# Controller feed-forward: tie test, pick product and output product each moved within and across the steps of a software pipeline

## The reference

```python
lr = xf @ m1                                            # 128 -> 64
mask_logits = jnp.einsum('bl,lxy->bxy', lr, m2) + mb    # 8 blocks x 64
quant_mask = jnp.argmax(mask_logits, axis=-1)           # one unit in each block
mid = jnp.einsum('ai,aji->aj', xf, w1p[j, quant_mask])
relu = jax.nn.relu(mid)
res = jnp.einsum('ai,aij->aj', relu, w2p[j, quant_mask]) + b2
# outside: x = x + tanh(g_ffn[2]) * res, with xf = layernorm(x)
```

## Time and profile before

| | |
|---|---|
| median of three runs | 1644.13 us (1643.41 to 1644.64) |
| the profiled execution | 1646.58 us |
| its span, first to last instruction | 1644.8 us |
| busy: PE, DVE, ACT, POOL | 1391.0, 1037.0, 716.7, 768.4 us |
| mean granted TensorE clock | 0.931 of full speed |

### The profile page before, as it was taken

One profiled execution on the slowest core, in us unless ns is written; L12 is line 12 of the kernel. 1 busy time (PEld: TensorE's weight loads), 2 busy tenths in 40 slices (PEclk: granted clock), 3 DMA queues, 4 the chain that ended last, 5 costly groups with the idle time before them and its releaser, 6 DMA issues. The chain is left out here.

```text
span 1644.8 us, 34070 instructions
## 1 busy us (share of the span) xinstructions
PE 1391.0 (85%) x10919; PEld 1114.0 (68%) x10919; DVE 1037.0 (63%) x2336; ACT 716.7 (44%) x1767; POOL 768.4 (47%) x989
## 2 busy tenths in 40 slices
PE   4998776989675877999978986999999999687996
PEld 3777556989565555666645546778788787486984
DVE  4887862414387787999958883545565754363555
ACT  2677453323365324565634442544545445221121
POOL 2554581444371444455434442445444676206445
PEclk9999997999856896999979997999999999898998
DMA  7400123758110000000000000000000000375952
GB/s 187 185 1 2 30 88 108 224 174 265 48 42 2 1 1 1 1 0 0 1 1 0 0 0 1 1 0 0 1 1 1 11 17 19 98 218 174 292 154 83
DMA packets 96485, 100.02 MB, mean 61 GB/s; under 512 B 12149, under 2 KB 69677, under 8 KB 95726
## 3 DMA queue, kind: packets, MB, share of 16 engines
q1 hardware_dynamic: 62322, 69.60, 14.0%
q0 software_dynamic: 8192, 16.79, 3.4%
q10 hardware_dynamic: 25852, 12.09, 2.6%
HBM read 72.23 MB, written 26.21 MB: 60 GB/s over the span
## 5 line engine op out<-in xcount | busy, mean ns | idle before, releaser
L445 POOL TENSOR_TENSOR exp_scores<-exp_scores,softmax_recip 128x308 f32<-128x308 f32 x256 | 181.8, 741 | 181.1 <-DVE softmax_recip L614 180.9
L640 PE MATMUL psum<-identity,exp_scores 128*77 128x128 f32 x1024 | 163.6, 286 | 34.2 <-POOL exp_scores L445 21.6
L1966 POOL TENSOR_TENSOR exp_scores_xattn<-exp_scores_xattn,softmax_recip_xattn 128x1640 f32<-128x1640 f32 x32 | 93.5, 2921 | 162.5 <-DVE softmax_recip_xattn L2139 162.5
L1211 PE MATMUL psum<-sorted_transposed_ffn,tile_weights_up_ffn 128*128 128x128 f32 x1280 | 164.2, 283 | 5.0 <-DVE sorted_transposed_ffn L1099 4.7
L1211 PEld LDWEIGHTS psum<-sorted_transposed_ffn,tile_weights_up_ffn 128*128 128x128 f32 x1280 | 153.8, 197 | 11.7 <-DVE sorted_transposed_ffn L1099 11.5
L640 PEld LDWEIGHTS psum<-identity,exp_scores 128*77 128x77 f32 x1024 | 122.5, 152 | 56.7 <-issue 26.3
L985 POOL DMA_INDIRECT gathered_rows_ffn<-sorted_y,slot_ffn x96 | 90.7, 945 | 104.3 <-DMA sorted_y<-expert_rows_ffn 45.7
L460 ACT COPY probs_transposed<-psum 77x512 f32<-77x512 f32 x192 | 111.1, 581 | 52.2 <-PE psum L640 50.6
L1221 PE MATMUL psum<-expert_weights_down_ffn,hidden_ffn 128*128 x960 | 124.4, 281 | 3.4 <-issue 2.8
L974 POOL DMA_INDIRECT sorted_x<-xn_ffn,slot_ffn x64 | 61.3, 958 | 132.3 <-DVE slot_ffn L859 113.4
L1221 PEld LDWEIGHTS psum<-expert_weights_down_ffn,hidden_ffn 128*128 128x128 f32 x960 | 116.6, 196 | 5.8 <-issue 5.8
(11 more groups left out here) (367 smaller groups left out, 3353.4 us busy)
## 6 DMA issues: line engine op xcount, KB each, us to landing
tile_weights_up_ffn<-in_L_ffn_packed_dram SPq DMA_DIRECT2D x160, 256.0 KB, 3.2
sorted_rows_ffn<-sorted_x SPq DMA_DIRECT2D x80, 128.0 KB, 3.5
sorted_y<-expert_rows_ffn ACTq DMA_DIRECT2D x80, 128.0 KB
sorted_x<-zeros SPq DMA_DIRECT2D x4, 1280.0 KB, 13.4
x_residual<-in_x_dram SPq DMA_DIRECT2D x4, 512.0 KB, 11.1
expert_weights_down_ffn<-in_L_ffn_packed_dram SPq DMA_DIRECT2D x8, 256.0 KB, 15.5
sorted_x<-xn_ffn,slot_ffn POOLq DMA_INDIRECT x128, 2.3
gathered_rows_ffn<-sorted_y,slot_ffn POOLq DMA_INDIRECT x128, 2.7
```

The lines of the kernel that those rows point to most:

```text
L445: nc.gpsimd.tensor_tensor(e[:, par, heads, :], e[:, par, heads, :], rec.to_broadcast([S, HG, KC]), ALU.mult).then_inc(s["probs_ready"], 1)
L640: last = nc.tensor.transpose(m.psum[0:KC, 4 + g % 2, h * S:(h + 1) * S], e[:, nxt, g * HG + h, :], m.ident[:, :])
L1211: mm = nc.tensor.matmul(m.psum[:, 2 * (n % 2) + half, to:to + SUB], w[:, n % DEPTH, u, at:at + 128], xst[:, n % 2, u * SUB:(u + 1) * SUB], ...
L1966: nc.gpsimd.tensor_tensor(ev, ev, recip[:, par, :].unsqueeze(2).to_broadcast([S, H3, KV]), ALU.mult).then_inc(s["probs_ready"], 1)
```

## The change

`pipeline_pairs` replaces `pipeline4` in this stage, and `has(b, lag)` says whether batch b - lag exists (always, in the loop); the loop now holds steps 4 to 27 and six steps are written out after it. In the step of batch b the parts are now: transpose, w1's product and low-rank product of b + 1; logits, top, comparison and count multiply of b; code, tie test and product of b - 1; transposes, `rt` copy, w2's product and addition of b - 2; statistics of b - 3. No instruction of a batch is added or removed.

The diff, cut to its core (the engines' loops; waits on buffers follow the new order):

```diff
+def has(b, lag):
+    return not isinstance(b, int) or 0 <= b - lag < B
...
@@ gpsimd
-                    if middle:
+                    if has(b, 0):
                         wait(pool, s["ge_ready"], b + 1)
...
@@ scalar
+                    if has(b, 2):
+                        wait(act, s["rt_in_psum"], b - 1)
+                        wait(act, s["y_done"], b - 2)
+                        nc.scalar.copy(rt[:, :], m.psum[:, 5, :]).then_inc(s["rt_ready"], 1)
...
-                    if back:
-                        wait(act, s["rt_in_psum"], b)
-                        wait(act, s["y_done"], b - 1)
-                        nc.scalar.copy(rt[:, :], m.psum[:, 5, :]).then_inc(s["rt_ready"], 1)
...
@@ vector
+                    if has(b, 0):
+                        wait(dve, s["logits_in_psum"], b + 1)
+                        wait(dve, s["ge_ready"], b)
+                        nc.vector.tensor_reduce(top[:, :], logits, AX.X, ALU.max).then_inc(s["top_ready"], 1)
+                    if has(b, 1):
                         wait(dve, s["coded"], b)
+                        wait(dve, s["first_ready"], b - 1)
                         nc.vector.tensor_reduce(code[:, :], pv, AX.X, ALU.max).then_inc(s["code_ready"], 1)
+                    if has(b, 0):
                         wait(dve, s["top_ready"], b + 1)
                         wait(dve, s["rt_in_psum"], b - 1)
                         nc.vector.tensor_tensor(pick[:, par, :, :], logits, top[:, :].unsqueeze(2).to_broadcast(wide),
                                                 ALU.is_ge).then_inc(s["ge_ready"], 1)
+                    if has(b, 1):
+                        wait(dve, s["code_ready"], b)
+                        nc.vector.tensor_tensor(pv, pv, code[:, :].unsqueeze(2).to_broadcast(wide), ALU.is_equal).then_inc(s["first_ready"], 1)
+                    if has(b, 3):
+                        statistics(b - 3)
+                    if has(b, 1):
                         wait(dve, s["first_ready"], b)
                         wait(dve, s["full_ready"], b)
                         nc.vector.tensor_tensor(pf, pf, full[:, nxt, :], ALU.mult).then_inc(s["picked_ready"], 1)
...
@@ tensor
+                    if has(b, 2):
+                        wait(pe, s["picked_ready"], b - 1)
+                        wait(pe, s["rt_ready"], b - 2)
+                        for c in range(CH):
+                            mm = nc.tensor.transpose(m.psum[:, 5, c * S:(c + 1) * S],
+                                                     pick[:, par, :, :].rearrange("p x y -> p (x y)")[:, c * 128:(c + 1) * 128], m.ident[:, :])
+                        mm.then_inc(s["rt_in_psum"], 1)
+                    if has(b, -1):
+                        wait(pe, s["xt_ready"], b + 2)
+                        wait(pe, s["full_ready"], b)
+                        nc.tensor.matmul(m.psum[:, 3 + nxt, :], xt[:, nxt, :], w1[:, :], start=True, stop=True).then_inc(s["full_in_psum"], 1)
+                        nc.tensor.matmul(m.psum[0:ML, 0, S:2 * S], m1[:, :], xt[:, nxt, :], start=True, stop=True).then_inc(s["low_in_psum"], 1)
+                    if has(b, 2):
                         wait(pe, s["rt_ready"], b - 1)
                         wait(pe, s["x_done"], b - 2)
...
```

More of the change, by code:

```diff
@@ L1711, in _, with pipeline_pairs @@
                 pipeline4(pe, step, NGB)
+def has(b, lag):
+    return not isinstance(b, int) or 0 <= b - lag < B
+def pipeline_pairs(eng, step, n=B):
+    for b in range(-1, 4):
+        step(b, b % 2)
+    with eng.Fori(0, (n - 8) // 2) as i:
+        step(i * 2 + 4, 0)
+        step(i * 2 + 5, 1)
+    for b in range(n - 4, n + 2):
+        step(b, b % 2)
 def controller_feed_forward(nc, m, sem, clear):
@@ L1756, in step @@
                                                 ALU.mult).then_inc(s["coded"], 1)
-                pipeline4(pool, step)
+                pipeline_pairs(pool, step)
             @block.scalar
@@ L1769, in normalise, with step @@
                                          bias=m.shift[:, bass.ds(b, 1)]).then_inc(s["xn_ready"], 1)
-                def step(b, par, front, middle, back, tail):
+                def step(b, par):
                     nxt = 1 - par
-                    if front:
+                    if has(b, -1):
                         wait(act, s["xt_in_psum"], b + 2)
@@ L1776, in step @@
                         nc.scalar.copy(xt[:, nxt, :], m.psum[:, 0, 0:S]).then_inc(s["xt_ready"], 1)
-                    if front and not (isinstance(b, int) and b + 2 >= B):
+                    if has(b, -2):
                         wait(act, s["xt_in_psum"], b + 1)
                         normalise(b + 2, par)
-                    if front:
+                    if has(b, 2):
+                        wait(act, s["rt_in_psum"], b - 1)
+                        wait(act, s["y_done"], b - 2)
+                        nc.scalar.copy(rt[:, :], m.psum[:, 5, :]).then_inc(s["rt_ready"], 1)
+                    if has(b, -1):
                         wait(act, s["low_in_psum"], b + 2)
@@ L1787, in step @@
                         nc.scalar.activation(full[:, par, :], m.psum[:, 3 + par, :], ACT.Relu).then_inc(s["full_ready"], 1)
[L1788 to L1791 removed]
                 normalise(0, 0)
[L1794 removed]
+                pipeline_pairs(act, step)
                 preload(nc, m, ACT.Sqrt)
@@ L1803, in _, with statistics, step @@
                 wide = [S, MX, MY]
-                def step(b, par, front, middle, back, tail):
+                def statistics(b):
+                    wait(dve, s["x_done"], b + 1)
+                    nc.vector.bn_stats(m.moments[:, b, :], m.x[:, b, :])
+                def step(b, par):
                     nxt = 1 - par
-                    pv = pick[:, nxt, :, :]
-                    if back:
+                    logits, pv = m.psum[:, 1 + par, :].rearrange("p (x y) -> p x y", y=MY), pick[:, nxt, :, :]
+                    if has(b, 0):
[3 more added lines that the diff above has]
+                    if has(b, 1):
                         wait(dve, s["coded"], b)
+                        wait(dve, s["first_ready"], b - 1)
                         nc.vector.tensor_reduce(code[:, :], pv, AX.X, ALU.max).then_inc(s["code_ready"], 1)
[L1812 to L1819, removed]
+                    if has(b, 0):
                         wait(dve, s["top_ready"], b + 1)
@@ L1833, in step @@
                                                        ALU.mult, ALU.add).then_inc(s["x_done"], 1)
-                        wait(dve, s["x_done"], b - 1)
-                        nc.vector.bn_stats(m.moments[:, b - 2, :], m.x[:, b - 2, :])
-                pipeline4(dve, step)
+                pipeline_pairs(dve, step)
+                statistics(B - 1)
             @block.tensor
@@ L1861, in step @@
                         mm.then_inc(s["y_done"], 1)
[L1862 to L1876, removed]
+                pipeline_pairs(pe, step)
 def latent_attention(nc, m, sem, r, clear):
```

9 lines of the change are left out of this document (3 added, 6 removed).

## The result

The kernel after takes 1658.45 us (median of 5 runs, 1653.07 to 1659.09) against 1644.13 (1643.41 to 1646.65): ratio 1.0078, 95% interval 1.0062 to 1.0094. It is slower by 14 us; the forecast was 1651.7, range 1645 to 1659. (In later runs the kernel before had medians of 1646.24 and 1647.78; against those the loss is 12 and 11 us.) The mechanism of the steady steps came out as forecast. The larger part of what the stage itself lost is TensorE's clock in the fill and the drain, where the forecast saw less of it or none. The start of the next stage took 2.1 us longer too, but no run ties that to the change.

A forecast was written before the change was run, and what follows sets the result against it. The prediction took the closed ring of VectorE and GpSimd waits, 4.255 us a step, to bound the kernel. Fill +4.1, steps +2.7 and drain +0.8 gave +7.6 on 1644.13, thus 1651.7 us, range 1645 to 1659.

The forecast's parts named there:

- The mechanism of the steady steps: Steady steps: VectorE's product, with two SBUF inputs, waits 1.00 us for GpSimd's multiply; 28 steps give +2.7.
- The ring: Steady step, VectorE and GpSimd waiting for each other: 4.255 us becomes 4.35, +2.7 over 28 steps, bounds 0 to +5.6.
- The faster rival: Steady step: VectorE isn't held, GpSimd pays for both, TensorE's 3.9 bounds; -9.9 in the steps, 1638.3 us, chance 0.12.
- The much slower rival: Steady step: GpSimd's bias addition gets ahead of the waiting product, holding it 0.42 longer; step 4.77, 1664 us, chance 0.08.
- The fill: Stage start to comparison of batch 3: bare w1's product, uncovered copy waits and later clock rise, +4.1, bounds +2.4 to +7.2.
- the one that let the clock rise halfway through TensorE's fourth step: Fill: TensorE's step after batch 2's logits runs half at half clock and takes 3.7 + 1.9 us.
- The drain: Last comparison to end of last statistics: last code starts behind held product and addition, one statistics intervenes; +0.8, 0.5 to 1.2.
- The total: Whole kernel: fill, steps and drain sum to +7.6, giving 1651.7 us, range 1645 to 1659 for 8 in 10.

The follow-up runs named there:

- Experiment 1: Kernel after with ReLU and product fused into one VectorE instruction reading PSUM, three banks for w1's products: 1646.51 us, ratio to before 0.9992.
- experiment 8: Kernel after with VectorE's old order alone put back, all else as in after: 1656.77 us, ratio 1.0062.
- Experiments 5: Kernel after with idle identity products on TensorE at the stage's start, in the fill and in the drain: 1644.70 us, ratio to before 0.9992.
- experiment 6: Kernel before with idle identity products on TensorE at the stage's start and in the fill, none in the drain: 1642.20 us, ratio 0.9979.
- experiment 4: Kernel after with idle identity products on TensorE during its waits in the last three steps: 1657.07 us, ratio 1.0071.
- experiments 2: Kernel before with ReLU and product fused into one VectorE instruction reading PSUM, two banks as before: 1639.44 us, ratio 0.9967.
- experiment 7: Kernel after with fused product from PSUM, low-rank product ahead of w1's, and fewer idle identity products in fill and drain: 1631.34 us, ratio to before 0.9905.
- experiment 3: Kernel after with the low-rank product put back ahead of w1's product on TensorE: 1652.05 us, ratio 1.0048.

## Why the prediction was right, and where it fell short

**The ring: right.** The forecast had the product wait 1.00 for GpSimd's multiply and end 0.55 after it; it ends 0.54 after it and lasts 1.55. Experiment 1 takes the second SBUF input away and the product takes 0.67 beside the same multiply, experiment 8 lets it start ahead of the multiply and it takes 0.68, so the cause is shown and not only argued. The step was forecast at 4.35 and measured at 4.325: 28 steps cost 1.95 instead of 2.7, inside the bounds 0 to 5.6. The hold costs the 0.87 us by which the product grew. By the Trainium skill (SBUF — State Buffer, section "Who interferes with whom") this is the port pair that VectorE and GpSimd share. The trace agrees: the product takes 1.55 when GpSimd's multiply has begun before it, and 0.68 when it begins before the multiply.

**The faster rival: wrong, but its price was right.** No product row in the loop is near 0.68 with a multiply over 2 us. Where the product was freed (experiment 1), TensorE did bound, at 3.914 where the forecast had 3.9 for it.

**The much slower rival: wrong.** GpSimd's bias addition did not get ahead of the waiting product. It paid itself: 0.90, where the earlier trace rows have 0.45.

**The fill: right kind, too small.** Forecast +4.1, measured +5.9, within 2.4 to 7.2. The order of events was right: w1's product bare in front of the first logits, two gaps of 0.35 in each step, and a clock that stays low for longer. The step of it that failed is the one that let the clock rise halfway through TensorE's fourth step, 5.6 us long: that step ran at half clock nearly to its end (862) and took 7.03. The steps ahead of it took 5.68 instead of 5.53. Together that is 1.4 + 0.3, nearly all of the 1.8 missing. Experiments 5 and 6 give the split: 1.0 us is the deeper pipeline, 4.9 the clock.

**The drain: mis-sized.** Forecast +0.8, bounds 0.5 to 1.2, measured +3.3. The 0.8 was right for a full clock: with it the difference is 0.75 (experiments 5 and 6). What failed is a silent assumption, that the clock stays up as in before. TensorE waits 1.83 for the product of batch 30, the clock falls towards the end of that wait (0.86 from 988 to 988.5, then 0.50), and w2's products and the transposes pay 2.6 (experiment 4). A held product is not needed for that: in experiment 8, where this product takes 0.68, TensorE waits nearly as long and the clock falls too (0.78 from 990 to 991, then 0.50):

```profile
989.27 0.66 PE L1876 MATMUL psum<-identity,pick_ffn 128*128 128x128 f32 x4 [1.75 <-DVE pick_ffn L1847]
```

The product comes behind the last comparison, and in the new order TensorE has nothing else left then. In the kernel before, its last two waits for a product are 0.89 and 0.81.

**The next stage: not in the sum, and not shown to belong to the change.** The forecast ended the account at the last statistics; the preparation behind them took 2.1 us longer. It starts at half clock in after (0.50) and at full clock in before (1.00), but that cost nothing: the first product that needs the transposed weights starts 9.15 behind the end of the statistics in both (987.40 in before, 996.88 in after).

```profile
996.55 3.78 PE L2177 MATMUL psum<-weights_transposed_xattn 128*128 128x128 f32 x16 [5.82 <-DVE bv_wide_xattn L2064]
```

```profile
1006.03 3.79 PE L2194 MATMUL psum<-weights_transposed_xattn 128*128 128x128 f32 x16 [3.46 <-DVE bv_wide_xattn L2081]
```

The 2.1 come later, as the clock falls and rises again within the stage: the 16 products of L_wo that follow, for instance, take 3.22 in after and 2.05 in before. They go neither with the order nor with the clock in the drain: the same preparation takes 28.22, 27.88 and 27.90 in experiments 2, 4 and 7, whose clock is at 1.00 to the end of the drain, and 26.19 in experiment 3, whose drain is at half clock. What decides it is open.

**The total: inside the range in part by luck.** 1658.45 lies 0.6 under the upper end. The drain went 2.1 over its bound and the next stage was not in the sum at all; the range held because the steps took 1.95 of the 5.6 that it allowed them, and the fill 5.9 of 7.2. Of the 14.3 between the medians, 1.0 lies in no milestone.

## What to carry to other kernels

When an instruction is moved behind another, ask what GpSimd does at its new place: with two SBUF inputs a VectorE instruction waited there for the whole rest of GpSimd's, and with one input in PSUM it did not. Count a pipeline's fill and drain at the clock that TensorE will have there: of the 11.2 us that this stage lost, 7.5 were the clock (4.9 in the fill, 2.6 in the drain). Look at the start of the next stage apart: here it took 26.2 or about 28 us in either order. Idle products on a waiting TensorE are a cheap way to tell a long fill from a slow clock, and may be worth leaving in, as experiment 7 does.

## What was unexpected

The clock differed at the same place with the same code near it. The kernel before and that of experiment 6 reach the first scores of the next stage within 0.1 us of each other (start, duration):

```profile
1013.60 4.89 PE L2206 MATMUL psum<-kv_transposed_xattn,queries_xattn 128*128 128x205 f32 x16 [0.78 <-DVE queries_xattn L2144]
```

```profile
1013.69 3.04 PE L2215 MATMUL psum<-kv_transposed_xattn,queries_xattn 128*128 128x205 f32 x16 [0.78 <-DVE queries_xattn L2153]
```

The same 16 products take 4.89 in the one and 3.04 in the other; the granted clock from 1012 to 1016 was 0.50 (1.2 GHz) and 0.81. In the profiled runs of these ten kernels the rest of the span, with the same code, took 1467.8 to 1477.0 us; part of it is this. It is why the milestones were trusted above the medians where a few us mattered, and it may be why the kernel before spans 1642.87 to 1650.93 in 23 runs; only one of these executions has a trace. What decides which of the two a run gets was not tried.

GpSimd's next instruction, queued while VectorE's is held, also paid: the bias addition took 0.90 behind the held product and 0.45 where the product read PSUM.
